# Expert rows fetched from ScalarE's queue, late fetches ahead of stores, and eight output buffers for four

## The reference

```
logits = flat @ Wr
top_vals, top_idx = top_k(logits, 2)
top_w = softmax(top_vals)
for e in range(8):
    hdn = gelu(flat @ W1[e] + b1[e])          # 128 -> 512
    y = hdn @ W2[e] + b2[e]                   # 512 -> 128
    out = out + gates[:, e:e + 1] * y
t = t + out                                   # then back to images
```

## Time and profile before

| | us |
|---|---|
| median of 3 runs | 748.9 |
| lowest and highest | 744.53 and 751.57 |
| profiled execution | 745.43 |
| its span, first to last instruction | 743.6 |

### The profile page before, as it was taken

How to read it: one execution, slowest core, us unless ns; L and a number is a source line. 1 busy time by engine, 2 the same in 40 slices (tenths; PEclk the granted TensorE clock), 3 DMA queues, 4 the chain that set the end, 5 groups by cost and what they waited for, 6 DMA issues and landing times.

```text
span 743.6 us, 20844 instructions
## 1 busy us (share of the span) xinstructions
PE 620.5 (83%) x6696; PEld 488.2 (66%) x6696; DVE 563.2 (76%) x1755; ACT 480.5 (65%) x940; POOL 455.6 (61%) x482
## 2 busy tenths in 40 slices
PE   1586878888887888889749899999999999998753
PEld 1244545555554555555428898989999999997642
DVE  6667989999987899989866778656666666665765
ACT  1256768777776677877638866767777777774400
POOL 7000026676665566577777577777777777764571
PEclk9989999999998999999959999999999999999955
DMA  5754485555645555553244445664445454489796
GB/s 141 221 154 133 115 207 165 173 160 177 180 124 155 163 179 179 152 151 109 72 104 96 88 93 93 132 128 102 101 101 107 96 105 93 95 203 240 240 288 241
DMA packets 138769, 108.84 MB, mean 146 GB/s; under 512 B 100339, under 2 KB 121367, under 8 KB 138674
## 3 DMA queue, kind: packets, MB, share of 16 engines
q1 hardware_dynamic: 122450, 76.74, 42.3%
q0 software_dynamic: 13056, 26.02, 12.2%
q10 hardware_dynamic: 3168, 4.82, 1.8%
HBM read 45.26 MB, written 42.85 MB: 118 GB/s over the span
## 4 chain that ended last, share of the span: by engine, by line
PE 41%; DVE 22%; DMA 15%; ACT 7%; SPq 6%; issue 5%; POOL 2%; DVEq 0%; POOLq 0%; ACTq 0%
PE pair_d L1002 14%; PE pair_b L985 7%; PE pair_c L985 7%; DMA conv_planes<-conv_y 6%; PE pair_a L783 4%; DMA out<-seen_g 3%; DMA conv_y<-conv_planes 3%; DVE xb_x L1688 3%; DMA fld<-dispatched_rows 2%; PE pair_c L869 2%; SPq L489 2%; DVE p_area L1435 2%; ACT p_area L1105 1%; DVE w L1515 1%; DVE st L1355 1%
## 5 line engine op out<-in xcount | busy, mean ns | idle before, releaser
L645 POOL DMA_INDIRECT dispatched_rows<-p_area,pos x198 | 198.4, 1002 | 108.1 <-issue 53.7
L716 POOL DMA_INDIRECT expert_rows<-conv_y,dest x210 | 205.7, 980 | 83.9 <-issue 54.5
L1002 PE MATMUL pair_d<-w,xb_x 128*128 x2520 | 168.5, 220 | 0.0
L1002 PEld LDWEIGHTS pair_d<-w,xb_x 128*128 128x128 f16 x2520 | 152.7, 98 | 2.7
L1701 DVE TENSOR_TENSOR conv_y<-pair_d,share 128x256 f32<-128x256 f32 x105 | 44.5, 424 | 71.3 <-PE pair_d L1002 68.9
L985 PE MATMUL pair_b<-xrt,w 128*128 128x256 f16 x636 | 79.6, 276 | 12.4 <-DVE xb_x L1688 9.9
L783 PE MATMUL pair_a<-conv_y,p_area 128*32 128x392 f16 x1152 | 64.7, 366 | 22.4 <-DMA conv_y<-conv_planes 17.9
L1207 ACT ACTIVATE xb_x<-pair_b 128x512 f16<-128x512 f32 x106 | 57.6, 596 | 37.7 <-PE pair_d L1002 35.5
L985 PE MATMUL pair_c<-xrt,w 128*128 128x256 f16 x624 | 78.1, 276 | 0.1
L1207 ACT ACTIVATE xb_x<-pair_c 128x512 f16<-128x512 f32 x104 | 56.5, 596 | 32.0 <-PE pair_d L1002 32.0
L1688 DVE TENSOR_TENSOR xb_x<-pair_b,xb_x 128x512 f16<-128x512 f32 x106 | 68.0, 683 | 10.6 <-ACT xb_x L1207 10.5
(11 more groups left out here) (279 smaller groups left out, 1145.5 us busy)
## 6 DMA issues: line engine op xcount, KB each, us to landing
conv_y<-conv_planes SPq DMA_DIRECT2D x64, 225.0 KB, 3.9
xb_x<-in_x SPq DMA_DIRECT2D x32, 392.0 KB, 4.4
p_area<-expert_rows SPq DMA_DIRECT2D x11, 784.0 KB, 9.9
conv_planes<-conv_y SPq DMA_DIRECT2D x32, 225.0 KB
t_all<-p_area SPq DMA_DIRECT2D x16, 392.0 KB
out<-seen_g ACTq DMA_DIRECT2D x12, 392.0 KB, 7.7
t_all<-in_L_ffn_W SPq DMA_DIRECT2D x16, 256.0 KB, 5.1
expert_rows<-conv_y,dest POOLq DMA_INDIRECT x210
```

What stands on the lines that cost most here:

```text
L645: pool.indirect_dma_start(xs, bass.IndirectOffsetOnAxis(ap=pos[0:m, u, t, k:k + 1].bitcast(U32), axis=0), rows[0:m, u, t, :].bitcast(U32), ...
L716: pool.indirect_dma_start(ys, bass.IndirectOffsetOnAxis(ap=dest[:, place, slot, s:s + 1].bitcast(U32), axis=0), y[:, t % STORE_DEEP, s, :] ...
L1002: last = T.matmul(dst, ghl[:, t % 2, gp, f * TILE + s * P:f * TILE + (s + 1) * P], w2[:, wp, bass.ds(w0 + f * P, P)], start=False, stop=(f ...
```

## The change

FETCH_AT is now an iteration of ScalarE's loop: it waits for the stores of the first 88 tiles and then issues the seven early fetches, one behind its work in each iteration from 91 on. SyncE's loop has none left. Behind its loop the order is: image 7, store 0, image 8, store 1, image 9; when the last hidden layer is made, images 10 and 11, store 2; when image 3 is turned, image 12, store 3; then as before. Images 10, 11 and 12 change buffers for this. The early combination starts at iteration 93 in place of 92, so that the turn of image 3 comes behind the last output, and its last addition behind the loop. Four more output buffers lie where the hidden activations and the images were (`xb_x1`); an addition waits for the store of the image eight before it.

```diff
-ROW_BUFFER_OF = (0, 1, 2, 3, 4, 5, 6, 0, 1, 2, 3, 7, 8, 9, 10, 4)
+ROW_BUFFER_OF = (0, 1, 2, 3, 4, 5, 6, 0, 1, 2, 7, 8, 3, 9, 10, 4)
-COMBINED, COMBINE_AT, COMBINE_EVERY = 4, 92, 3
-FETCH_AT, FETCHED_AMONG = 96, 7
+OUT_BUFFER_OF = (0, 1, 2, 3, 4, 5, 6, 7, 0, 1, 2, 3, 4, 5, 6, 7)
+COMBINED, COMBINE_AT, COMBINE_EVERY = 4, 93, 3
+FETCH_AT, FETCHED_AMONG = 91, 7
...
+        o_late = xb_x1[:, 0:SUM_DEEP * L].rearrange("p (u l) -> p u l", u=SUM_DEEP)
...
+        def out_of(i):
+
+            b = OUT_BUFFER_OF[i]
+            return o[:, b, :] if b < SUM_DEEP else o_late[:, b - SUM_DEEP, :]
+
+        def outs_before(i):
+
+            return 16 * OUT_BUFFER_OF[:i].count(OUT_BUFFER_OF[i])
...
                 load_tile(t)
-                if t == FETCH_AT:
-                    for b in range(STORE_BATCHES):
-                        sp.wait_ge(S[f"stored_{b}"], 32 * store_uses(b, KNOWN))
-                if FETCH_AT <= t < FETCH_AT + FETCHED_AMONG:
-                    load_y(t - FETCH_AT)
-
-            for i in range(COMBINED):
+
+            for b in range(STORE_BATCHES):
+                sp.wait_ge(S[f"stored_{b}"], 32 * store_uses(b, KNOWN))
+            for i in range(2):
                 sp.wait_ge(S["yt_ready"], i + 1)
-                load_y(FETCHED_AMONG + i)
-                if i < COMBINED - 1:
-                    store_out(i)
+                load_y(sp, 7 + i)
+                store_out(i)
+            sp.wait_ge(S["yt_ready"], 3)
+            load_y(sp, 9)
             sp.wait_ge(S["h_ready"], 2 * TILES)
-            for i in (11, 12):
-                load_y(i)
-            store_out(COMBINED - 1)
+            load_y(sp, 10)
+            load_y(sp, 11)
+            store_out(2)
+            sp.wait_ge(S["yt_ready"], 4)
+            load_y(sp, 12)
+            store_out(3)
...
                     gate_tanh(q, half)
+                if t == FETCH_AT:
+                    for b in range(STORE_BATCHES):
+                        act.wait_ge(S[f"stored_{b}"], 32 * store_uses(b, KNOWN))
+                if FETCH_AT <= t < FETCH_AT + FETCHED_AMONG:
+                    load_y(act, t - FETCH_AT)
...
-                    if some(16 * (i // SUM_DEEP)):
-                        dve.wait_ge(S[f"out_{i % SUM_DEEP}"], 16 * (i // SUM_DEEP))
+                    if some(outs_before(i)):
+                        dve.wait_ge(S[f"out_{OUT_BUFFER_OF[i]}"], outs_before(i))
...
-            combine_early(TILES)
+            for t in range(TILES, COMBINE_AT + COMBINE_EVERY * (COMBINED - 1) + 5):
+                combine_early(t)
```

More of the change, by code:

```diff
@@ L262, in build @@
             "dest_ready", "y_ready", "y_copied", "stored_0", "stored_1", "stored_2", "stored_3",
-            "yl_loaded_0", "yl_loaded_1", "yl_loaded_2", "yl_loaded_3", "yl_loaded_4", "yl_loaded_5", "yl_loaded_6", "yl_loaded_7", "yl_loaded_8", "yl_loaded_9", "yl_loaded_10", "ysum_ready", "ysum_pool", "yt_ready", "o_ready", "out_0", "out_1", "out_2", "out_3",
+            "yl_loaded_0", "yl_loaded_1", "yl_loaded_2", "yl_loaded_3", "yl_loaded_4", "yl_loaded_5", "yl_loaded_6", "yl_loaded_7", "yl_loaded_8", "yl_loaded_9", "yl_loaded_10", "ysum_ready", "ysum_pool", "yt_ready", "o_ready", "out_0", "out_1", "out_2", "out_3", "out_4", "out_5", "out_6", "out_7",
         )}
@@ L273, in rows_of, with load_y @@
             return over_w1[:, b - 7] if b < 9 else over_w2[:, b - 9]
+        y_img = ys.rearrange("(b p r) d -> b p (r d)", b=IMAGES, p=TT)
+        def load_y(eng, i):
+            eng.dma_start(rows_of(i).rearrange("p t k d -> p (t k d)"), y_img[i]).then_inc(S[f"yl_loaded_{ROW_BUFFER_OF[i]}"], 16)
         def loads_of(i):
             return 16 * ROW_BUFFER_OF[:i + 1].count(ROW_BUFFER_OF[i])
+        def out_of(i):
[3 more added lines that the diff above has]
+            return 16 * OUT_BUFFER_OF[:i].count(OUT_BUFFER_OF[i])
         def sums_before(i, owned):
@@ L498, in place_pad @@
                 sp.dma_start(xs[bass.ds(place, TILE), :].rearrange("(s p) c -> p s c", p=P), pad_rows[:, :, :].bitcast(U32)).then_inc(S["padded"], 16)
-            y_img = ys.rearrange("(b p r) d -> b p (r d)", b=IMAGES, p=TT)
-            def load_y(i):
-                sp.dma_start(rows_of(i).rearrange("p t k d -> p (t k d)"), y_img[i]).then_inc(S[f"yl_loaded_{ROW_BUFFER_OF[i]}"], 16)
             def store_out(i):
                 sp.wait_ge(S["o_ready"], i + 1)
-                sp.dma_start(out_img[i], o[:, i % SUM_DEEP, :]).then_inc(S[f"out_{i % SUM_DEEP}"], 16)
+                sp.dma_start(out_img[i], out_of(i)).then_inc(S[f"out_{OUT_BUFFER_OF[i]}"], 16)
             sp.wait_ge(S["tables_early"], 1)
@@ L546, in _ @@
             for i in (13, 14):
-                load_y(i)
+                load_y(sp, i)
             sp.wait_ge(S["yt_ready"], 5)
-            load_y(15)
+            load_y(sp, 15)
         @block.gpsimd
@@ L1235, in _ @@
                     gate_tanh(q, half)
+                if t == FETCH_AT:
[3 more added lines that the diff above has]
+                    load_y(act, t - FETCH_AT)
             for i in range(COMBINED, IMAGES):
                 act.wait_ge(S["o_ready"], i + 1)
-                act.dma_start(out_img[i], o[:, i % SUM_DEEP, :]).then_inc(S[f"out_{i % SUM_DEEP}"], 16)
-            for u in range(SUM_DEEP):
-                act.wait_ge(S[f"out_{u}"], 16 * IMAGES // SUM_DEEP)
+                act.dma_start(out_img[i], out_of(i)).then_inc(S[f"out_{OUT_BUFFER_OF[i]}"], 16)
+            for u in range(2 * SUM_DEEP):
+                act.wait_ge(S[f"out_{u}"], 16 * OUT_BUFFER_OF.count(u))
         @block.vector
@@ L1710, in add_rows @@
                     dve.wait_ge(S["yt_ready"], i + 1)
-                    if some(16 * (i // SUM_DEEP)):
-                        dve.wait_ge(S[f"out_{i % SUM_DEEP}"], 16 * (i // SUM_DEEP))
-                last = V.tensor_tensor(o[:, i % SUM_DEEP, :].rearrange("p (q t) -> p t q", t=NT)[:, t0:t1], sum_pair(i)[:, 0:NT * P].rearrange("p (t k) -> p t k", k=P)[:, t0:t1, 0:TT],
+                    if some(outs_before(i)):
+                        dve.wait_ge(S[f"out_{OUT_BUFFER_OF[i]}"], outs_before(i))
+                last = V.tensor_tensor(out_of(i).rearrange("p (q t) -> p t q", t=NT)[:, t0:t1], sum_pair(i)[:, 0:NT * P].rearrange("p (t k) -> p t k", k=P)[:, t0:t1, 0:TT],
                                        t2_all[:, i * L:(i + 1) * L].rearrange("p (t k) -> p t k", k=TT)[:, t0:t1], ALU.add)
```

## The result

The change makes the kernel slower: 758.9 us median of 4 runs (752.49 to 763.97) against 749.39 for the kernel before on the same chip, ratio 1.012, 95% interval 1.0065 to 1.0175. Run again later beside other kernels it had a median of 754.6 us and a ratio of 1.0055 (1.0006 to 1.0104). Every ratio leaves out the runs that are over 1.5% above the fastest of their kernel, so it isn't the quotient of the medians given, which are of all runs. The forecast was 738.5.

A forecast was written before the change was run, and what follows sets the result against it. Bound: TensorE to 656 us, then the DMA engines, behind the loop a GpSimd and SyncE chain. Gains 4.1 + 1.5 + 1.3 + 1.7 = 8.6 us off 745.43 gave 736.8; 1.8 added for run spread, 738.5; range 727 to 748.

The forecast's parts named there:

- So the two queues are served in the order of issue, as one: Loop: tile loads on SyncE's queue still stand behind fetches moved to ScalarE's; only the order within a tile changes.
- The DMA work of this stage is what it is; the change doesn't remove a byte: Stage from 656.73 us, given to the DMA engines: 4.0 us for each fetch with its tile, unchanged by the change.
- The term for the loop: Early fetches on ScalarE: first wait for fields grows 0.3 us, second or slow tile gains 1.8, together 1.5 gained.
- Eight buffers: Behind the loop: two waits for stores, 10.9 us, go; sum of image 15 then awaits its fetch, gaining 4.1 us.
- The 6.8 us: Behind the loop: further gain at VectorE's sum of image 15, to be had only by issuing its fetch earlier.
- Early sums one tile later: End of the loop: last outputs come some 2 us forward, of which 1.3 us counts, bounds 0 and 2.
- late fetches ahead of stores: Behind the loop: last stores of expert rows land in 5.0 us, not 6.7, gaining 1.7; bounds 0 and 4.4.
- Where the fetches stand: Loop: first early fetch issued 1.1 to 3.2 us later than before, 1.1 taken; ScalarE's issues of 0.34 to 0.36 us cost nothing.
- C: Rival, loop: small tile-load packets each wait for a 7 KB fetch packet; gain 5.0 us, 742.2 us; chance 0.09.
- D: Rival, ScalarE: its sequencer is held at each fetch issue, delaying gelus; 11.7 us slower, 758.9 us; chance 0.07.
- A: Rival, loop: tile loads pass the fetches, both waits for fields and the slow clock go; gain 17.0, 730.2 us; chance 0.12.
- B: Rival, behind the loop: last fetches come no earlier, only the buffers' 4.1 us are left; 743.1 us; chance 0.18.

The follow-up runs named there:

- e12: Changed kernel, early fetches still on ScalarE, with token rows from tile 96 on loaded plainly, not turned by the load (other numbers result): ratio 0.9904.
- e13: Changed kernel with the seven early fetches back on SyncE and token rows from tile 96 on loaded plainly, not turned: ratio 0.9917.
- e3: Kernel before with one edit, eight output buffers in place of four: 746.88 us, ratio 0.997.
- e1: Changed kernel with the seven early fetches back on SyncE, one behind the loads of each tile from 96 to 102: 744.24 us, ratio 0.9925.
- e11: Changed kernel with the seven early fetches on ScalarE issued behind two tiles in three, from 91 to 100: ratio 0.9951.
- e4: Changed kernel with each early fetch, still on ScalarE's queue, cut into seven transfers of 1 KB a row: 746.78 us, ratio 1.0012.
- e7: Changed kernel with each early fetch, on ScalarE, in two transfers of 4 KB and 3 KB a row: ratio 1.0017.
- e8: Changed kernel with the early fetches whole on ScalarE, one behind every second tile from 91 to 103: ratio 0.9928.
- e10: Changed kernel with fetches 0 to 4 on ScalarE behind every second tile from 91 to 99, 5 and 6 on SyncE behind the loop: ratio 0.9918.
- e9: Changed kernel with early fetches on SyncE, images 0 to 4 behind every second tile from 96, 5 and 6 behind the loop: 739.19 us, ratio 0.9869.

## Why the prediction was wrong

**The step that failed** is "So the two queues are served in the order of issue, as one", with what it carries, "The tile loads will stand behind the fetches as before". It was read from the earlier trace rows, where ScalarE's stores got no packet beside SyncE's fetches. In that stretch no load turns anything. Whether show order of issue at all the runs leave open. With plain loads, e12 and e13, the time is the same whichever queue the fetches are on, though in e12 the packets of the two queues alternate; with turning loads the step is false in the time as well. Behind it stands a second sentence, "The DMA work of this stage is what it is; the change doesn't remove a byte". True of the bytes; the time for them rose by 40% in one execution (254 over 181) and by 22% in the other (254 over 208). The term for the loop was +1.5 with bounds -1.1 and 9.9; it measured -6.0 and -10.9. The lower bound held only a later start, and no lower throughput.

**Eight buffers, 4.1.** Right in size, and by e3 in what is late next, the fetch of image 15. The 6.8 us that VectorE was to have in hand ahead of it are not there: in e3 it waits 0.98 us for the rows of one late image and 0.41 for those of image 15. One of its sums took 5.93 us in place of 1.07; what held it comes next.

**Early sums one tile later, 1.3, and late fetches ahead of stores, 1.7.** e1 has both and e3 neither. The last stores do land sooner: in e1 SyncE's wait ends at 724.0, 4.6 us after GpSimd's last store, at 719.39; forecast 5.0. But GpSimd ends 55.5 us after the issue of tile 96 in e1, 54.7 in e3 and 55.6 before, so the earlier outputs bring nothing in these executions. And VectorE in e1, 715 us to the end, hardly waits any more:

```profile
DVE seen_g L1731 <- PE pair_a L1046: 0.4, 1, 0.4
DVE xb_x L1731 <- PE pair_d L1046: 0.3, 1, 0.3
```

That doesn't make VectorE the bound. One of its sums stands in the trace with 5.91 us, where the others take 1.06 to 1.08, and beside it stand sums of GpSimd, one behind the other since 719.39:

```profile
724.68 5.91 DVE L1724 TENSOR_TENSOR w<-w 112x896 f32<-112x896 f32 x1
...
725.53 2.08 POOL L749 TENSOR_TENSOR w<-w 112x896 f32<-112x896 f32 x1
727.57 2.07 POOL L749 TENSOR_TENSOR p_area<-p_area 112x896 f32<-112x896 f32 x1
```

The last of these ends at 729.64, VectorE's sum 0.95 us later, which is about what a sum takes by itself. In all twelve traces with eight output buffers in which VectorE reaches a sum while GpSimd's run, it ends 0.95 to 0.97 us behind the run of them. VectorE's additions beside the same sums take their usual 1.6 us. So a sum of VectorE waits for GpSimd's sums, and the view of waits doesn't list it. That makes GpSimd the bound behind the loop: 6.2 us from the last gated output to the end of its stores, 10.3 for five sums, 0.95 for VectorE's sum, then 16.3 for its further sums and additions and the last store. That is 33.7 us, alike in after, its second execution, e1 and e11 to e13, with loops from 49.3 to 61.6 us. In e1 the rows of image 15 land 3.0 us ahead of their sum (724.89 + 10.8 against 738.67): so much of an earlier fetch couldn't be used. What the kernel gains when these sums don't meet was not tried.

Of the 3.0 us some 0.9 is left by the traces (83.9 us from the issue of tile 96 to the end in e3, 83.0 in e1), less than these executions differ among themselves. The runs leave it open: e1's median is 2.6 us below e3's on the same chip, and the intervals of the two ratios overlap.

**Where the fetches stand.** ScalarE issues the first 4.27 us after SyncE's load of tile 96 (661.99 - 657.72), against 2.03 before: 2.2 later, within the 1.1 to 3.2 given. Issues took 0.31 to 0.35 us, as said. The gap came ahead of the fourth fetch, not the fifth, and was 16 us, not 4, since ScalarE's tanh waits for the same fields.

**The rivals.** C had the direction: loads held up by fetches. It is the rule that the Trainium skill states ("DMA: Bandwidth & Descriptors", section Queues, rings and completion order), turns by whole packets between queues with work. e4 agrees with it: with smaller packets on ScalarE's queue the fields come through. The turns in e12 agree with it too; e7, where packets of half the size take nothing off the wait, does not. But the rule gives no reason for fewer bytes per second, 181 GB/s against 254, and e12, where rows of 7 KB are still on another queue and no time is lost, shows that it alone doesn't make the loss. C also let the second wait go; it was 7.0 us. D's 758.9 is the measured median by coincidence: its mechanism, an issue held at ScalarE, is absent. A and B did not come about.

The Trainium skill, same page, section Rules for kernel authors, says that a transpose next to ordinary DMAs needs nothing. That is said of results. For time the table of four above differs: such neighbours cost 1.3 to 2% of this kernel.

## What to carry to other kernels

A transfer that is moved to another engine's queue is not only issued elsewhere: here the DMA engines moved 254 GB/s with both streams on one queue and 181 to 208 with large reads on a second queue beside turning loads. Before moving it, look in the trace for a stretch with the same kinds of transfers on both queues; one with other kinds, as the earlier trace rows, doesn't answer. And where a stage is short of DMA time, spacing the fetches that nobody awaits yet (every second tile) brought back here as much as the move back to SyncE did: 0.9928 and 0.9918 (e8, e10) against 0.9925 (e1). Both together had 0.9869 (e9), with an interval that overlaps with these. Last, a view of waits doesn't show an instruction that is held while it runs: compare its duration with that of its like.

## What had not been expected of the hardware

- DMA share near 1 tells nothing of throughput: 0.98 goes with 91 GB/s and 0.99 with 308, 4 us apart in one execution.
- A 3 KB transfer took 15.23 us to land, and SyncE's issue of a transposing load 4.45 us, beside three fetches on another queue. Plain loads are not free of that: in e12 one issue of fields took 5.15 us, at 684.22, beside the fetches.
- Cut into 1 KB parts, six issues on ScalarE took up to 4.08 us, 0.68 each, where single ones of 7 KB a row took 0.31: issuing is no longer free when there are many.
- A sum of VectorE that takes 1.07 us by itself took 3.9 to 8.45 us when it began while GpSimd's sums ran, and always ended about 0.95 us behind the last of them.
